# Two wide attentions in one software-pipelined stage, and a packed last chunk in the MLP of a small decoder

## The reference, cut to what matters

```python
x = _layernorm(x + _L0_attn_ref(x, ...))      # softmax(q k^T) v, heads of width 256, rotary tables
x = _layernorm(x + _L0_xattn_ref(x, ctx, ctx, mask, ...))   # the same on ctx_1024, masked and causal
x = _layernorm(x + _L0_ffn_ref(x, ...))       # 8 experts, the best 2 of each token
x = _layernorm(x + _L1_attn_ref(x, ...))      # 16 heads of width 16
x = _layernorm(x + _L1_xattn_ref(x, ...))
x = _layernorm(x + _L1_ffn_ref(x, ...))

def _L1_ffn_ref(x, ...):
    for i in range(6):
        x = attn_layer(shift_tokens(x), ...) + x     # 16 heads of 64, windows of 64, look back one
        x = ffn_layer(shift_tokens(x), ...) + x

def ffn_layer(x, g, bln, W1, b1, W2, b2):            # W1: 256 x 1364, W2: 682 x 256
    hg = layernorm(x) * g + bln @ W1 + b1
    a, gate = split(hg)                              # 682 columns each
    return a * gelu(gate) @ W2 + b2
```

## Time and profile before

| | |
|---|---|
| time of three runs | 4715.07 us median, 4713.5 to 4718.72 |
| the profiled execution | 4714.29 us; span from first to last instruction 4712.5 us |
| busy share of the span | TensorE 94%, VectorE 63%, ScalarE 56%, GpSimd 25% |
| wide attention, first to last | 49.8 to 384.6 us |
| expert layer and head attentions | 384.6 to about 1623 us |
| `stage_l1_ffn` | about 1623 to 4680 us, 124.7 us a body |

### The profile page before, as it was taken

The page is one execution under the profiler, slowest core; times in us unless marked ns, Lnnn a source line. Parts: engine busy times, 40 slices in busy tenths (PEclk is TensorE's granted clock), DMA queues, the critical chain, the costliest instruction groups (busy, mean ns, idle before and its releaser), DMA issues. The chain is left out here.

```text
span 4712.5 us, 87906 instructions
## 1 busy us (share of the span) xinstructions
PE 4406.3 (94%) x31376; PEld 2762.0 (59%) x31376; DVE 2949.1 (63%) x10294; ACT 2639.7 (56%) x6827; POOL 1190.7 (25%) x757
## 2 busy tenths in 40 slices
PE   4778999898999899999999999999999999999995
PEld 2445666565666555666666666666666666666663
DVE  1341222377777687777777777777777777777762
ACT  1221222366666567666666666666666666666660
POOL 0000000000000054333333333333333333333320
PEclk9998999999999999999999999999999999999997
DMA  4000000100000100010101110111001100110001
GB/s 153 7 20 0 0 0 0 52 2 4 17 22 8 42 21 19 20 46 24 37 19 47 28 35 17 47 28 37 17 21 44 39 21 20 46 34 27 19 15 38
DMA packets 78629, 128.54 MB, mean 27 GB/s; under 512 B 13858, under 2 KB 48404, under 8 KB 77844
## 3 DMA queue, kind: packets, MB, share of 16 engines
q1 hardware_dynamic: 78228, 123.28, 9.0%
HBM read 68.74 MB, written 4.19 MB: 15 GB/s over the span
## 5 line engine op out<-in xcount | busy, mean ns | idle before, releaser
L454 PE MATMUL psum<-f_wqkv,f_xsT 128*128 128x512 f32 x2304 | 1075.1, 595 | 4.1 <-ACT f_raw L591 2.7
L806 POOL TENSOR_TENSOR f_raw<-f_rot 128x512 f32<-128x512 f32 x384 | 487.4, 1269 | 1776.2 <-DVE f_rot L666 1776.2
L605 ACT ACTIVATE f_prob<-f_prob,f_nb,f_rq 128x128 f32<-128x128 f32 x1536 | 740.2, 488 | 9.3 <-DVE f_nb L715 8.4
L707 DVE CUSTOM_DVE_ANT_0 f_prob<-psum,f_band 128x128 f32<-128x128 f32 x1536 | 355.8, 286 | 524.2 <-issue 410.1
L454 PEld LDWEIGHTS psum<-f_wqkv,f_xsT 128*128 128x128 f32 x2304 | 400.4, 191 | 322.1 <-issue 317.5
L553 PE MATMUL psum<-f_xnT,f_w 128*128 128x512 f32 (+1 forms) x1152 | 526.8, 597 | 1.9 <-ACT f_xnT L626 1.1
L811 POOL TENSOR_TENSOR f_rn<-f_ss,f_half_pow 128x32 f32<-128x32 f32 x96 | 522.2, 5439 | 11.2
L589 ACT ACTIVATE f_sq<-psum 128x512 f32<-128x512 f32 x384 | 229.4, 597 | 254.5 <-PE psum L454 254.4
L730 DVE TENSOR_SCALAR f_prob<-f_prob,f_rs 128x128 f32<-128x128 f32 x1536 | 351.6, 292 | 13.7 <-DVE f_rs L724 0.2
L553 PEld LDWEIGHTS psum<-f_xnT,f_w 128*128 128x128 f32 (+1 forms) x1152 | 198.2, 179 | 276.2 <-issue 273.6
L571 ACT COPY f_pT<-psum 128x512 f32<-128x512 f32 x192 | 111.5, 581 | 434.3 <-PE psum L434 434.3
(11 more groups left out here) (226 smaller groups left out, 7879.9 us busy)
## 6 DMA issues: line engine op xcount, KB each, us to landing
f_v_near<-f_v SPq DMA_DIRECT2D x168, 256.0 KB, 3.7
f_wqkv<-in_Wqkv SPq DMA_DIRECT2D x36, 512.0 KB, 5.8
w_moe_W<-in_L_ffn_W SPq DMA_DIRECT2D x2, 4096.0 KB
f_w<-in_W SPq DMA_DIRECT2D x6, 1364.0 KB, 5.6
f_wo<-in_Wo SPq DMA_DIRECT2D x6, 1024.0 KB, 6.6
f_xs<-x_all SPq DMA_DIRECT2D x24, 254.0 KB
h_mask_int<-in_mask_BxSxS_ik SPq DMA_DIRECT2D x16, 256.0 KB, 2.6
f_w<-in_W SPq DMA_DIRECT2D x6, 640.0 KB
```

The costliest lines, as they stand in the source:

```text
L454: mm = nc.tensor.matmul(ps.ap(step), xsT[:, c, t * P:(t + 1) * P], wqkv[:, c, i * HALF:(i + 1) * HALF], start=c == 0, stop=c == KC - 1)
L605: ex = nc.scalar.activation(pr, pr, ACT.Exp, bias=nb[:, t % 2, h:h + 1], scale=rq8[:, t, h:h + 1], accum_out=sums[:, t % 2, h:h + 1])
L707: red = nc.vector.tensor_tensor_reduce(prob[:, (4 * n + 2 * j + i) % 16, :], ps.ap(key)[:, j * P:(j + 1) * P], band[:, min(t, 1), :], 1.0, ...
L806: nc.gpsimd.tensor_tensor(raw[:, (4 * t + i) % 8, :], rot[:, n % 2, 0, :], rot[:, n % 2, 1, :], ALU.add).then_inc(rope_done, 1)
```

## The change

1. `stage_wide` replaces both calls of `stage_wide_attention`. Its eight bodies (four blocks of self attention, four of cross attention) are software-pipelined: body `it` does scores and outputs of block j and, between them, transposes and projections of block j+1. The products q, k and v have two buffers. ScalarE copies `pt` n-1 before the exponential of n. The residual is added in place in `x_all`, and the copies `xin`, `xb` and `y` are gone. The mask of the next cross block is built at the end of slot 3.
2. The weight loads move from the first block of code into SP's part of `stage_wide`; of `x` only the first block is loaded ahead, the rest after the weights of `a0`. The other engines wait for what they need.
3. In `stage_l1_ffn` the last chunk of 42 value units and the last of 42 gate units are packed into one chunk of 128 columns (values at PSUM rows 0 to 41, gates at 64 to 105, zeros between): step `f1p` in place of the two products `f1g` 5 and `f1a` 5. ScalarE's Gelu moves the gates down to rows 0 to 41. A new VectorE step `f1b`, first in slot 15, multiplies them, even tiles into rows 0 to 41 and odd tiles into rows 64 to 105 of `hT`.
4. The `f2` of two tiles stand behind each other (slots 1 and 5, none in 2 and 6). The five full chunks run as before; the last chunks of both tiles are issued together after the odd tile's, in rows 0 to 42 and 64 to 106, into two banks. `W2`'s last rows and `b2` are loaded twice for this.
5. `xt` reads `x_all` itself; the copy `xin` on GpSimd and the two unused `sem_inc` are gone. W1 is loaded in three pieces instead of one, after a memset of the gaps on VectorE, and the loads of a layer's MLP weights are 8 and 5 DMAs, where 5 and 3 were.

```diff
@@ load_w1, load_w2
-        sp.dma_start(self.w1[:], w["W1"][l].rearrange("(c p) n -> p c n", p=P)).then_inc(self.w1_landed, 16)
+        source, full, W = w["W1"][l].rearrange("(c p) n -> p c n", p=P), (self.HC - 1) * P, P // 2
+        sp.dma_start(self.w1[:, :, 0:self.HID], source[:, :, 0:self.HID]).then_inc(self.w1_landed, 16)
+        sp.dma_start(self.w1[:, :, full + P:], source[:, :, self.HID:self.HID + full]).then_inc(self.w1_landed, 16)
+        sp.dma_start(self.w1[:, :, full + W:full + W + self.HREM], source[:, :, self.HID + full:]
+                     ).then_inc(self.w1_landed, 16)
...
+        for row in (0, P // 2):
+            sp.dma_start(self.w2[row:row + self.HREM, self.HC - 1, :], w["W2"][l][full:self.HID]
+                         ).then_inc(self.w2_landed, 16)
...
@@ body() of stage_l1_ffn
+                if n == N - 1:
+                    yield ("f1b", -1)
...
-                    1: [("f2", -2, 0)], 2: [("f2", -2, 1)], 3: [("wo", -1, 3)],
-                    4: [("xin", 1), ("tab", 1, 0)], 5: [("f2", -2, 2)], 6: [("f2", -2, 3)],
+                    1: [("f2", -2, 0), ("f2", -2, 1)], 3: [("wo", -1, 3)],
+                    4: [("tab", 1, 0)], 5: [("f2", -2, 2), ("f2", -2, 3)],
...
-                    14: [("f1g", -1, 4), ("f1g", -1, 5)],
-                    15: [("f1a", -1, 4), ("f1a", -1, 5), ("wo", 0, 2)]}.get(n, ())
+                    14: [("f1g", -1, 4), ("f1p", -1)],
+                    15: [("f1a", -1, 4), ("wo", 0, 2)]}.get(n, ())
@@ SyncE
+            sp.wait_ge(gaps_cleared, 1)
             weights.load_w1(sp, 0)
             weights.load_w2(sp, 0)
             sp.dma_start(before, x_all[:]).then_inc(saved, 16)
@@ TensorE
+                    elif kind == "f1p":
+                        pe.wait_ge(ps.sem_drained(step), ps.before(step, it))
+                        for c in range(KC):
+                            mm = nc.tensor.matmul(ps.ap(step), w1[:, c, (HC - 1) * P:HC * P], xnT[:, c, :],
+                                                  start=c == 0, stop=c == KC - 1)
+                        mm.then_inc(ps.sem_filled(step), 1)
...
-                        for c in range(HC):
-                            m = P if c < HC - 1 else HREM + 1
-                            mm = nc.tensor.matmul(ps.ap(step)[:, 0:D], hT[0:m, c, t * P:(t + 1) * P],
-                                                  w2[0:m, c, :], start=c == 0, stop=c == HC - 1)
-                        mm.then_inc(ps.sem_filled(step), 1)
+                        for c in range(HC - 1):
+                            nc.tensor.matmul(ps.ap(step)[:, 0:D], hT[:, c, t * P:(t + 1) * P], w2[:, c, :],
+                                             start=c == 0, stop=False)
+                        if t % 2:
+                            for n in (t - 1, t):
+                                rows = slice(n % 2 * W, n % 2 * W + HREM + 1)
+                                key = ("f2", off, n)
+                                nc.tensor.matmul(ps.ap(key)[:, 0:D], hT[rows, HC - 1, n * P:(n + 1) * P],
+                                                 w2[rows, HC - 1, :], start=False, stop=True
+                                                 ).then_inc(ps.sem_filled(key), 1)
@@ ScalarE and VectorE
+                    elif kind == "f1p":
+                        wait_filled(act, ps, step, it)
+                        nc.scalar.activation(hT[0:HREM, HC - 1, :], ps.ap(step)[W:W + HREM], ACT.Gelu,
+                                             bias=weights.b1g_last[W:W + HREM, HC - 1:HC]).then_inc(gate_ready, 1)
...
+                    elif kind == "f1b":
+                        key = ("f1p", off)
+                        dve.wait_ge(gate_ready, it + off + 1)
+                        values = ps.ap(key).rearrange("p (t q) -> p t q", q=P)
+                        packed = hT[:, HC - 1, :].rearrange("p (t q) -> p t q", q=P)
+                        for odd in range(2):
+                            tiles = slice(odd, TB, 2)
+                            ins = nc.vector.scalar_tensor_tensor(
+                                out=packed[odd * W:odd * W + HREM, tiles], in0=values[0:HREM, tiles],
+                                scalar=b1a[0:HREM, HC - 1:HC], in1=packed[0:HREM, tiles], op0=ALU.add, op1=ALU.mult)
+                        ins.then_inc(ps.sem_drained(key), 1)
@@ stage_wide
+            early = {0: [("xt", 1, 0), ("xt", 1, 1)], 1: [("q", 1, 1)], 2: [("k", 1, 1)], 3: [("v", 1, 1)]}
+            late = {0: [("q", 1, 0)], 1: [("k", 1, 0)], 2: [("v", 1, 0)], 3: []}
+            for n in range(TB):
+                off = -1 if n == 0 else 0
+                yield from [("s", 0, n), ("max", 0, n), ("pt", off, n - 1), ("e", 0, n), *early[n],
+                            ("pv", off, n - 1), *late[n]]
+                if n == 1:
+                    yield from [("ln", -1), ("bias", 1)]
+                if n == 2:
+                    yield ("norm", -1)
+                if n == 3:
+                    yield ("mask", 1)
@@ mk_decoder
+            def load_later(sp, load_source):
+                for st in ORDER:
+                    for of, dst, src in loads:
+                        if of == st:
+                            sp.dma_start(dst, src).then_inc(landed[st], 16)
+                    if st == "a0":
+                        sp.dma_start(x_all[:, S // P:, :], x_tiles[:, S // P:, :]).then_inc(landed["x_rest"], 16)
+                    elif st == "x0":
+                        load_source(0)
...
-            stage_wide_attention(nc, shared, "a0", a0, rope, cross=False)
-            stage_wide_attention(nc, shared, "x0", x0, None, cross=True)
+            stage_wide(nc, shared, a0, x0, rope, load_later)
```

More of the change, by code:

```diff
@@ L311, in stage_l1_ffn @@
                 banks[("o",) + step[1:]] = 7
-            elif kind in ("qkv", "wo", "f2", "f1g", "f1a"):
+            elif kind in ("qkv", "wo", "f2", "f1g", "f1a", "f1p"):
                 banks[step] = (0, 1, 6)[ring["p"] % 3]
@@ L442, in _ @@
                         c = step[2]
-                        pe.wait_ge(xin_ready, it + off + 1)
-                        transposes(step, it, [(t, xin[:, t, c * P:(c + 1) * P]) for t in range(TB)])
+                        pe.wait_ge(x_ready, it + off + 1)
+                        transposes(step, it, [(t, x_all[:, tile(it + off, t), c * P:(c + 1) * P]) for t in range(TB)])
                     elif kind == "qkv":
@@ L920, in stage_wide_attention @@
         rs_ready = sem("rs_ready")
[L921 to L932 removed]
+        biased = sem("biased")
@@ L933, in stage_wide_attention @@
+        full = list(body())
+        banks, ring = {}, 0
+        for step in full:
             kind = step[0]
-            if kind in banks:
-                for i in range(2):
-                    ps.fill(step + (i,), banks[kind][i])
+            if kind in ("xt", "pt"):
+                banks[step] = 2 + ring % 2
+                ring += 1
             elif kind == "s":
-                ps.fill(step, 4 + step[1] % 2)
-            elif kind == "pt":
-                ps.fill(step, 0 + step[1] % 2)
+                banks[step] = 4 + step[2] % 2
@@ L941, in stage_wide_attention, with cross, present @@
             elif kind == "pv":
-                ps.fill(step, 6 + step[1] % 2)
-        ps.finish(shared, NB)
+                banks[step] = 6 + step[2] % 2
+            elif kind in ("q", "k", "v"):
+                banks[step] = step[2]
+        def cross(j):
+            return j >= NB
+        def present(step, it):
+            j = it + step[1]
+            return 0 <= j < BODIES and (cross(j) or step[0] != "mask")
+        phases, ps = [], None
+        for it in range(-1, BODIES + 1):
+            ps = Psum(shared, it, ps, True)
+            steps = [step for step in full if present(step, it)]
+            for key, bank in banks.items():
+                if present(key, it):
+                    ps.fill(key, bank)
+            ps.finish(shared, 1)
+            phases.append((steps, ps, it))
@@ new lines, in _ @@
+                        c = step[2]
+                        if c == 0:
+                            if cross(j):
+                                pe.wait_ge(x_ready, j - NB + 1)
+                            elif j == 0:
+                                pe.wait_ge(shared["x_first"], 32)
+                            elif j == 1:
+                                pe.wait_ge(shared["x_rest"], 16)
+                        empty(step, it)
+                        for t in range(TB):
+                            mm = nc.tensor.transpose(ps.ap(step)[:, t * P:(t + 1) * P],
+                                                     x_all[:, tile(j, t), c * P:(c + 1) * P], ident[:])
@@ L1102, in _ @@
-            with dve.Fori(0, NB) as it:
+            dve.wait_ge(w_self["landed"], w_self["loads"])
+            for name in ("Wq", "Wk"):
+                plain = w_self[name + "_plain"][:].rearrange("p c (e two) -> p c e two", two=2)
```

(3 more changed lines are left out.)

534 lines of the change are left out of this document (280 added, 254 removed).

## The result

The changed kernel takes **4530.12 us** (median of four runs, 4529.56 to 4535.23) against 4715.69 for the kernel before on the same chip: ratio 0.961, 95% interval 0.959 to 0.963. The forecast was 4522, with a range of 4497 to 4566. The profiled execution took 4530.23 us with a span of 4528.4; the span of the kernel before was 4712.5, so the two traces differ by 184.1 us.

| stretch | forecast | measured |
|---|---|---|
| start to the expert stage's first transposes | -128 | 384.62 to 261.81: -122.8 |
| expert and head stages | 0 | -2.95 |
| from there to the end | -78.7 + 11 + 3 = -64.7 | -58.3 |

A forecast was written before the change was run, and what follows sets the result against it. TensorE's instruction list was taken to bound the MLP stage, the chain of waits the wide attentions. Terms -128 (wide), -78.7 (MLP products), +11 (short slots), +3 (MLP start) gave -193: 4522 us, range 4497 to 4566.

The forecast's parts named there:

- Start: Wide stage: `a0` landed at 13 us (bounds 11 and 20), first `s` at 27.3.
- A self body: Wide stage: 26.7 us of TensorE instructions, some 0.1 of waiting in slot 0; four such bodies, 107.
- Bodies 4 to 6: Wide bodies behind a mask: `q` 0 waits 2.6 us; three bodies at 29.4, together 88.
- First MLP product: MLP slot 15 loses `f1a` 5: -2.04 us a body; slot 14 unchanged, `f1b` free.
- Second: Second MLP product: two tails issued together run side by side, -0.62 us a pair, -1.24 a body.
- Short slots: MLP slots 2 and 6: TensorE waits 0.2 us at `xnt`, 0.3 at `wo`; 0.5 a body, +11.
- Start of the MLP stage: Loads wait for VectorE's memsets: about +3 us; five more DMAs hidden, +2.5 if uncovered.
- rival 1: MLP tail pair does not run side by side: 4537 us with half overlap, 4552 with none; chance 0.13.
- (2): MLP short slots cost nothing, later slots taking up VectorE's lag: 11 us better, 4511; chance 0.17.
- (3): MLP short slots cost three times as much, 1.5 us a body: 4544; chance 0.12.
- (4): Wide stage still waits on its chain, 5 us a body in all eight: 4554; chance 0.13.
- (5): MLP weight reloads: packed W1 piece delays TensorE, 39 us at each of five cancels the gain; chance 0.01.

The follow-up runs named there:

- experiment 11: The changed kernel with all weight loads issued in the first block of code, as before: 4567.01 us (0.969).
- experiment 6: The changed kernel with the pairs of the second MLP product in slots 2 and 6 in place of 1 and 5: 4520.14 us (0.958).
- wide_only: The wide stage and the loads of the changed kernel, with the MLP stage of the kernel before: 4591.58 us (0.974).
- experiment 8: The changed kernel with the next cross block's mask built right behind the maximum of slot 3, ahead of VectorE's evacuation: 4524.67 us (0.959).
- experiment 5: The changed kernel with the second MLP product in slots 1, 2, 5 and 6 as before, each tile with its own tail: 4546.79 us (0.964).
- experiment 10: The changed kernel with ScalarE's order as before, the exponential of tile n ahead of the copy of `pt` n-1: 4576.73 us (0.971).

## Why the prediction was right, and where it was off

It was 8 us low. Against the two traces the wide stage was 5.2 worse than forecast and the MLP stage 6.4, and 2.95 came back in stages that no one had changed, which is luck. Step by step:

- **Start.** `a0` landed at 13.6 (forecast 13). The first `s` was 2.8 late, 2.15 of it the held VectorE operation: the forecast had priced all four at 0.42, though the trace of the kernel before shows such an operation held. The worth of the early loads was right (experiment 11).
- **A self body.** Forecast 26.8, measured 27.24: the second `xt` waits 0.29 for the copy of `pt` (six times in the stage, 1.8 in all); what the rest is stays open. The first body has no `pt` and no `pv` ahead of `q` 0, so nothing covers the chain from the maximum over the exponential to `xT`. The forecast took it for a body like the others and gave it no wait; it had one of 1.92. The two errors cancel: at full clock it takes 26.71 (in the traces of experiment 6 and of `wide_only`). The 28.41 of the changed kernel is this and 1.70 for a stretch at the lower clock behind the wait, as in eight other traces.
- **Bodies 4 to 6.** Forecast 29.4, with 2.6 of waiting at `q` 0 behind the mask. The place was right: `q` 0 stands 7.43 into the body (forecast 7.5), but TensorE was free for it at 5.44, not 4.9, so the wait is 2.0. (The forecast's 1.75 from the maximum to the exponential is 1.79 in the earlier trace rows; it changes nothing.) Without the lower clock a body takes 29.47, and two of the three pay 1.7 more for it: 31.17, 31.17, 29.47. That it was the mask is shown by experiment 8.
- **The last body.** 23 forecast, 23.0 measured (232.04 to 255.04); the 2 added for the lower clock didn't come. The tail was 6.8 for 7.2.
- **Together.** The steps gave -130 and the forecast took -128; it was -122.8 in this trace: 2.8 at the start, 3.1 in the self bodies, 3.8 in bodies 4 to 6, less 2.0 in the last body and 0.4 in the tail. Of this 5.1 is TensorE's lower clock, at a place for which the forecast had nothing. In the trace of `wide_only` the same stage gave -128.0.
- **First MLP product.** -2.04 forecast, -2.04 measured; slot 14 +0.03. `f1b` at nothing is right.
- **Second.** -0.62 a pair forecast, -0.63 measured: the four records lie side by side. The reading by strict program order, with half an overlap, would have 0.92 and is refuted by 0.70 against 1.13. What the forecast put together as one tail of 0.63 is two things: two spacings (0.43), and changes of shape (0.20).
- **Short slots.** Forecast 0.2 at `xnt` and 0.3 at `wo`, measured 0.17 and 0.35, and 0.07 in slot 7 that it had not named: 0.6 in place of 0.5 a body, 2 us in all. Experiments 5 and 6 show the cause.
- **Start of the MLP stage.** +3 forecast, +3.28 in the wait; the first load stands 4.9 after the last normalisation where it stood 1.7 after it, and `x_before_mlp` lands 8.4 after its issue in place of 10.2, so the five further DMAs are hidden as forecast.
- **Filling and emptying.** The forecast multiplied 3.28 by 24, less 22 short slots. With the measured 0.62 (the 0.03 of slot 14 among it) that is -65.1 from the first `s` to the end; it was -62.4. The 2.7 are missing outside the steady bodies. In the last full body, where the projections of the next are missing, slots 7 to 9 take 20.83 us for 18.83, 1.8 more than the 0.24 that the short slots cost there in the other bodies; with the pairs in slots 2 and 6 (experiment 6) they take 18.80, so this too is the short slot 6. The other 0.9 stays open; 0.5 of it lies in the first body, which takes anything from 95.4 to 98.4 us over the 14 traces. The first `s` of the stage comes 4.1 later after the last normalisation, not 3.
- **Between.** The -2.95 in the expert and head stages come with TensorE's lower clock, as no step was changed there: the 33.1 us from the first heads on have a granted clock of 0.90 in the trace of the kernel before and of 1.00 in that of the changed one. From the first heads to the last normalisation it is 2.5 us longer at 0.90 in three of the 14 traces, that of experiment 10 among them, than at 1.00 in the other eleven. So these 2.95 are not a gain of the change.
- **The rivals.** The pair did run side by side (rival 1). The short slots cost 0.6 a body, neither nothing (2) nor 1.5 (3); at nothing they stand only with the pairs in slots 2 and 6. The wide stage waits on its chain in four bodies and not in eight, at 2 us and not 5 (4). The packed piece of W1 held nothing up: each of the 21 full bodies has the same length, those with the reloads too (5).

## What to carry to other kernels

In a software-pipelined list, merging two steps leaves one slot long and one short. Put the long one right ahead of the step that needs the other engines' results: the same work in slots 1 and 5 or in 2 and 6 differed by 0.58 us a body. Do not leave two short slots in a row without trying it: a second one behind the first cost 1.2 more here. Work that an engine need not do between the scores and their maximum, like the mask, belongs where that engine waits anyway; the idle bracket of the rows around it shows where. And before a gain of a few microseconds is believed or given up, compare the stages that were not changed: here they moved by 4 us by themselves.

## What was not expected of the hardware

- VectorE's TENSOR_TENSOR on two operands in SBUF, started while GpSimd's TENSOR_TENSOR was running, was not done until that had ended: 2.56 us for 0.42 at the start, in all nine traces in which the two met, and 0.42 in the three in which the addition came later; 1.39 for 0.68 in the MLP stage, 100 times, before and after the change. VectorE's TENSOR_SCALAR and its operations with an operand in PSUM kept their 0.75 and 0.48 beside GpSimd's addition in the cross bodies. The Trainium skill, SBUF — State Buffer, section "SBUF: two separate sides", calls the port pair that the two engines share an exclusive lock, held for a whole instruction by the one that starts first, and counts among those that take it an operation of VectorE with two SBUF inputs, against one of GpSimd that reads SBUF. The traces agree: 2.56 for 0.42. The forecast should have priced it.
- Two float32 products in rows 0 to 42 and 64 to 106 take 0.70 us together, as long as one alone, and their passes alternate.
- A change between 128 and 43 rows has a price of its own: two tails of which the first stands among 128-row products and the second ahead of `pv` cost 0.39 us more than two behind one another in the same rows.
- Behind a wait of 2 us ahead of `q` the granted clock fell from 2.4 to 1.2 GHz for part of the body (mean 0.95) in two of the three bodies behind a mask, and not in the third; in `wide_only` in one of the three. Without the wait it stayed at 1.00 in all three bodies of experiment 8. What decides whether it falls is not shown.
